# A conv block and a mixture of experts on one core: expert 0 made the fixed first place, its weights split ahead, tile 0 gathered by mask matmuls from rows in SBUF

## What is computed

```python
x = x + conv_block(ln_c(x))       # 8 x 256 x 16 x 16; groups of 8 channels: gates, 3x3 conv, FFT magnitude, sigmoid
t = to_tokens(x)                  # 2048 tokens x 256
xt = ln_t(t)
S = sigmoid(xt @ Wg)              # 2048 x 8
G, I = top_k(S, 2)
h = gelu(xt @ W1[e] + b1[e])      # 256 -> 1024, for each token's two experts e
y = h @ W2[e] + b2[e]             # 1024 -> 256
t = t + sum over the two experts of G * y
```

## Time and profile before

| | us |
|---|---|
| median of 3 runs (380.83 to 382.59) | 382.37 |
| the profiled execution | 382.42 |
| its span, first to last instruction | 380.2 |
| PE busy | 317.8 (84%) |
| DVE busy | 255.7 (67%) |
| ACT busy | 180.8 (48%) |
| POOL busy | 169.8 (45%) |

### The profile page before, as it was taken

How to read it: one execution, slowest core, us unless ns; L and a number is a source line. 1 busy time by engine, 2 the same in 40 slices (tenths; PEclk the granted TensorE clock), 3 DMA queues, 4 the chain that set the end, 5 groups by cost and what they waited for, 6 DMA issues and landing times.

```text
span 380.2 us, 8711 instructions
## 1 busy us (share of the span) xinstructions
PE 317.8 (84%) x3114; PEld 243.8 (64%) x3114; DVE 255.7 (67%) x572; ACT 180.8 (48%) x486; POOL 169.8 (45%) x145
## 2 busy tenths in 40 slices
PE   1899995999913109899999999999999999999960
PEld 1677631457713109788888888887888888888830
DVE  3986599437799552678878877887887656555640
ACT  3355583615429632654564466456456433442420
POOL 7023292514009451036456655654565555444331
PEclk9989998999955555999999999999999999999995
DMA  7300000001222986346676666767775444344221
GB/s 245 103 1 3 0 0 3 0 28 55 71 69 93 299 193 211 121 91 159 157 182 178 155 172 181 171 137 171 184 167 108 77 87 62 72 80 73 32 31 22
DMA packets 36696, 40.32 MB, mean 106 GB/s; under 512 B 8400, under 2 KB 33232, under 8 KB 36656
## 3 DMA queue, kind: packets, MB, share of 16 engines
q1 hardware_dynamic: 29168, 29.56, 27.2%
q0 software_dynamic: 7488, 10.23, 15.7%
HBM read 30.20 MB, written 9.57 MB: 105 GB/s over the span
## 4 chain that ended last, share of the span: by engine, by line
PE 47%; DMA 28%; DVE 11%; issue 4%; POOL 3%; ACT 3%; POOLq 0%; SPq 0%; ACTq 0%; DVEq 0%
DMA out<-fb,idx 21%; PE ps L839 9%; PE ps L828 5%; PE ps L832 5%; PE ps L830 5%; PE ps L840 5%; PE ps L673 4%; DMA fb<-xn_rows,idx 4%; POOL wt L437 3%; PE ps L693 3%; PE ps L702 2%; DMA xt<-x_tok 2%; PE ps L706 2%; PE ps L709 2%; DMA xn_rows<-wt 2%
## 5 line engine op out<-in xcount | busy, mean ns | idle before, releaser
L628 ACT ACTIVATE fb<-ps,b1t 128x128 f32<-128x128 f32 x312 | 84.7, 384 | 104.8 <-issue 101.5
L828 PE MATMUL ps<-fb,wt 128*128 128x128 f16 x624 | 121.9, 221 | 1.6 <-DVE fb L1202 1.6
L830 PE MATMUL ps<-fb,wt 128*128 128x128 f16 x624 | 121.9, 221 | 0.0
L832 PE MATMUL ps<-fb,wt 128*128 128x128 f16 x624 | 121.9, 221 | 0.0
L496 POOL DMA_INDIRECT out<-fb,idx x39 | 74.4, 1908 | 101.6 <-DMA out<-fb,idx 56.0
L839 PE MATMUL ps<-wt,fb 128*128 x312 | 117.5, 379 | 1.4 <-DVE fb L1202 1.4
L840 PE MATMUL ps<-wt,fb 128*128 x312 | 85.0, 273 | 0.0
L828 PEld LDWEIGHTS ps<-fb,wt 128*128 x624 | 61.8, 99 | 32.3 <-issue 1.8
L830 PEld LDWEIGHTS ps<-fb,wt 128*128 x624 | 61.8, 99 | 3.0
L832 PEld LDWEIGHTS ps<-fb,wt 128*128 x624 | 61.8, 99 | 0.0
L486 POOL DMA_INDIRECT fb<-xn_rows,idx x39 | 43.8, 1122 | 26.2 <-issue 9.8
(11 more groups left out here) (186 smaller groups left out, 401.4 us busy)
## 6 DMA issues: line engine op xcount, KB each, us to landing
wt<-w SPq DMA_DIRECT2D x32, 512.0 KB
b2t<-b SPq DMA_DIRECT2D x39, 128.0 KB
xt<-x_tok SPq DMA_DIRECT2D x4, 512.0 KB, 7.7
out<-xt SPq DMA_DIRECT2D x8, 256.0 KB, 2.1
xn_rows<-wt SPq DMA_DIRECT2D x8, 256.0 KB, 2.1
b1t<-params SPq DMA_DIRECT2D x39, 4.0 KB
fb<-xn_rows,idx POOLq DMA_INDIRECT x39
out<-fb,idx POOLq DMA_INDIRECT x39, 4.7
```

What stands on the lines that cost most here:

```text
L628: a = nc.scalar.activation(hid[:, s, f * P:(f + 1) * P], h_ps(s)[:, f * P:(f + 1) * P], ACT.Gelu_apprx_tanh, bias=b1t[:, n % NBIAS, f:f + ...
L828: pe.matmul(dst, hi, xT[:, s, c * P:(c + 1) * P], start=(c == 0 and f % 4 == 0), stop=False, skip_group_check=True)
L830: pe.matmul(dst, hi, xT[:, s, (2 + c) * P:(3 + c) * P], start=False, stop=False, skip_group_check=True)
L832: m = pe.matmul(dst, lo, xT[:, s, c * P:(c + 1) * P], start=False, stop=(c == DC - 1), skip_group_check=True)
```

## The change

- Expert 0 gets the highest sort key (`keybase`) and at least one tile, so place 0 is always expert 0, and tile 0 is always its first tile. Its four quarters and the biases of tile 0 are loaded at the start, from fixed addresses, and split in the conv stage. The second expert's first two quarters are split ahead of tile 0's gelu and of the gates' payload.
- The row blocks b = 0 and 1 are normalized inside the conv loop; the roots are taken in three parts (`ROWS_AT`) instead of two.
- Tile 0 is not gathered by DMA: DVE makes a mask per token block (`first`), PE multiplies the rows in SBUF by it, and the product is the transposed tile.
- `hot` and `pay` are made per block and choice by `tensor_scalar` with a scalar per partition; they are laid out so that PE reads 128 and 40 contiguous columns. Only one index table is made (40 columns instead of 80).
- The gate table moves from before step 0 to before step 2, `texp` gets a semaphore of its own, and POOL waits for `t_out` only before its first add.

```diff
-FIRST = SLOTS_MOST // P // E
+PLACE_FROM = [0] + [1 + -(-(SLOTS_MOST // P - 1) * p // (E - 1)) for p in range(E - 1)]
-QUARTERS_FIRST = QUARTERS
-QUARTERS_AHEAD = QUARTERS + 1
+QUARTERS_EARLY = QUARTERS + DC
-LATE_ROWS = B - 2
+ROWS_AT = [0, 3, B - 1, B]
+AHEAD = 4096.0
...
         def quarters_at(n):
-            first = QUARTERS_FIRST if n == 0 else n + QUARTERS_AHEAD
-            return range(first, min(n + QUARTERS_AHEAD + 1, NQ))
+            ahead = [4, 7, 8] + list(range(10, NQ + 1))
+            return range(ahead[n], ahead[n + 1]) if n + 1 < len(ahead) else range(0)
... SP
-            for b in range(B):
+            for h in range(QUARTERS):
+                load(h)
+            biases(0)
+            for b in range(B - 1):
                 sp.wait_ge(t_done, b + 1)
                 sp.dma_start(out_rows[:, 2 * b:2 * b + 2, :], xt[:, 2 * b:2 * b + 2, :]).then_inc(t_out, 16)
-            for b in range(B - NSTG + 1):
+            for b in range(B - 3):
                 rows_out(b)
+            sp.wait_ge(t_done, B)
+            sp.dma_start(out_rows[:, 2 * B - 2:2 * B, :], xt[:, 2 * B - 2:2 * B, :]).then_inc(t_out, 16)
             sp.wait_ge(perm_done, 1)
-            for h in range(NSTG):
+            for h in range(QUARTERS, QUARTERS_EARLY):
                 load(h)
-                if h + 1 < NSTG:
-                    rows_out(B - NSTG + 1 + h)
-            sp.wait_ge(table_done, 2)
-            for i in range(NBIAS):
+            for b in range(B - 3, B):
+                rows_out(b)
+            for h in range(QUARTERS_EARLY, 2 * QUARTERS):
+                load(h)
+            sp.wait_ge(texp_done, 1)
+            for i in range(1, NBIAS):
                 biases(i)
... POOL
-            g.tensor_scalar(by_row, c16[:, C16["iota"]].unsqueeze(2).broadcast_to([P, P, NBLK]), -1.0, 0.0,
-                            ALU.mult, ALU.add).then_inc(tables_set, 1)
-            for i in range(LEAD):
+            for i in range(1, LEAD):
                 gather(i)
... ACT
             deviation(grs[:, :], gmv[:, :, 1], eps_g, dev_g)
+            for h in range(DC):
+                split_hi(h)
...
             for u in range(B):
                 sigmoids(u)
                 if u in (0, 1, 4, 5):
                     shift(u + 4 if u < 2 else u + 2)
-            deviations(0, LATE_ROWS)
-            for b in range(LATE_ROWS - 1):
+                if DC <= u < QUARTERS:
+                    split_hi(u)
+                if u == B - 3:
+                    deviations(0)
+                if B - 3 <= u < B - 1:
+                    rows_hi(u - B + 3)
+            deviations(1)
+            for b in range(2, B - 1):
                 rows_hi(b)
-            deviations(LATE_ROWS, B - LATE_ROWS)
-            for b in range(LATE_ROWS - 1, B):
-                rows_hi(b)
+            deviations(2)
+            rows_hi(B - 1)
             act.wait_ge(logit_done, 2)
             nc.scalar.activation(sgl[:, :, :], lg[:, :, :], ACT.Sigmoid).then_inc(sigl_done, 1)
-            for h in range(QUARTERS_FIRST):
-                split_hi(h)
... PE
+            for k in range(NBLK):
+                if k % 4 == 0:
+                    pe.wait_ge(first_done, k // 4 + 1)
+                pe.wait_ge(xlo_done, k + 1)
+                for c in range(4):
+                    m = pe.matmul(ps[:, 0, c * P:(c + 1) * P], xrow[:, k, c * P:(c + 1) * P], first[:, k, :],
+                                  start=(k == 0 and c == 0), stop=(k == NBLK - 1), skip_group_check=True)
+            m.then_inc(xT_mm, 1)
-            table(0, 7)
-            pe.wait_ge(table_done, 2)
+            table(1, 1, 7)
...
-            turn(0)
-            load_expert(0)
-            table(2, 6)
+                if n == 0:                       # at the end of step(n)
+                    pe.wait_ge(texp_done, 1)
+                    load_expert(1)
+                    turn(1)
             for n in range(TILES + 2):
+                if n == 2:
+                    table(2, 2, 6)
                 step(n)
... DVE
+                if b < QUARTERS:
+                    split_lo(b)
                 if 2 <= b <= B:
                     add_x(b - 2)
                     stats_t(b - 2)
+                if b == B - 3:
+                    invert(0)
+            invert(1)
...
-            invert(0, LATE_ROWS)
             dve.wait_ge(prefix_mm, 1)
...
+            for k in range(NBLK):
+                ins = v.tensor_scalar(first[:, k, :], iota16, lowest[:, k:k + 1], None, ALU.is_equal)
...
             for a in range(TOP_K):
-                v.tensor_tensor(out=hot[:, a], in0=by_row, in1=place16[:, 0, a].unsqueeze(1).broadcast_to([P, P, NBLK]),
-                                op=ALU.is_equal).then_inc(hot_done, 1)
-            invert(LATE_ROWS, B - LATE_ROWS)
+                for k in range(NBLK):
+                    q = a * NBLK + k
+                    v.tensor_scalar(hot[:, q, :], iota16, minus_row[:, a, k:k + 1], 0.0, ALU.add, ALU.is_equal)
+                    ins = v.tensor_scalar(pay[:, q, 1, :], tiles16, tile_of[:, a, k:k + 1], cc("token")[:, k:k + 1],
+                                          ALU.is_equal, ALU.mult)
+                ins.then_inc(hot_done, 1)
+                if a == 0:
+                    invert(2)
+            rows_T(0)
             dve.wait_ge(table_mm, 1)
... idx, texp, scaled logits as before
-            for h in range(QUARTERS_FIRST):
+            for h in range(QUARTERS, QUARTERS_EARLY):
                 split_lo(h)
...
+            over_tiles = lambda n: place16[:, n].rearrange("p a k -> p (a k)").unsqueeze(2).broadcast_to([P, 2 * NBLK, TCOL])
+            link(v.tensor_tensor(out=pay[:, :, 0, :], in0=tiles16.unsqueeze(1).broadcast_to([P, 2 * NBLK, TCOL]),
+                                 in1=over_tiles(1), op=ALU.is_equal))
             for n in (2, 3):
-                ins = v.tensor_tensor(out=pay[:, n], in0=pay[:, 0], in1=over_tiles(place16[:, n]), op=ALU.mult)
+                ins = v.tensor_tensor(out=pay[:, :, n, :], in0=pay[:, :, 0, :], in1=over_tiles(n), op=ALU.mult)
```

More of the change, by code:

```diff
@@ L212, in build @@
         slot = sb("slot", [P, NBLK, E])
-        pick = view(1664, 2 * NBLK * E).rearrange("p (a k e) -> p a k e", a=2, k=NBLK)
+        pick, picked = [late[:, at:at + 2 * NBLK * E].rearrange("p (a k e) -> p a k e", a=2, k=NBLK) for at in (2880, 3136)]
         psum_pick = sb("picked", [P, 2, 2, NBLK])
@@ L216, in build @@
         place16 = sb("place16", [P, 4, 2, NBLK], F16)
-        tok16 = sb("tok16", [P, 2, NBLK], F16)
-        texpf = view(1920, TCOL * E).rearrange("p (i e) -> p i e", e=E)
+        keybase = sb("keybase", [P, E])
+        steps_of = view(4960, E * NBLK).rearrange("p (e k) -> p e k", k=NBLK)
+        lowest = view(5088, NBLK)
+        near, tile_of, minus_row = [view(at, 2 * NBLK).rearrange("p (a k) -> p a k", a=2) for at in (5104, 5136, 5168)]
+        texpf = late[:, 2560:2560 + TCOL * E].rearrange("p (i e) -> p i e", e=E)
         texpc = sb("texpc", [P, TCOL])
@@ L585, in rows_hi @@
             def rows_hi(b):
-                act.wait_ge(trs_done, 1 if b < LATE_ROWS else 2)
+                act.wait_ge(trs_done, 1 + (b >= ROWS_AT[1]) + (b >= ROWS_AT[2]))
                 for k in (2 * b, 2 * b + 1):
@@ L804, in step @@
                 one, two = n < TILES, n >= 2
-                if n % FIRST == 0 and n < FIRST * E:
-                    pe.wait_ge(lo_done, QUARTERS * (n // FIRST + 1))
-                if one:
+                for p in range(E):
+                    if n == PLACE_FROM[p]:
+                        pe.wait_ge(lo_done, QUARTERS_EARLY if p == 1 else QUARTERS * (p + 1))
+                if n == PLACE_FROM[1] + 2:
+                    pe.wait_ge(lo_done, 2 * QUARTERS)
+                e1 = e2 = 0
+                if one and n > 0:
                     e1 = pe.snap(expert[n % UNROLL], min_val=0, max_val=E - 1)
-                if two:
+                if n > 2:
                     e2 = pe.snap(expert[(n - 2) % UNROLL], min_val=0, max_val=E - 1)
@@ L818, in step @@
                 for f in range(FC):
-                    for c in range(DC if one else 0):
+                    for c in range(DC if one and n > 0 else 0):
                         pe.lower_ap(piece(e1, c * F + f * P + P - 1, 1))
                         pe.lower_ap(piece(e1, PIECE + c * F + f * P + P - 1, 1))
-                    if two:
+                    if n > 2:
                         pe.lower_ap(piece(e2, 2 * PIECE + f * 2 * C, 2 * C))
@@ L1071, in stats_t, with invert @@
                 ins.then_inc(var_t, 1)
-            def invert(b, n):
-                dve.wait_ge(dev_t, 1 if b == 0 else 2)
-                at = slice(2 * b, 2 * (b + n))
+            def invert(part):
+                dve.wait_ge(dev_t, part + 1)
+                at = slice(2 * ROWS_AT[part], 2 * ROWS_AT[part + 1])
                 link(v.reciprocal(trs[:, at], trs[:, at]))
@@ L1185, in _ @@
-            ins.then_inc(hot_done, 1)
+            slots = psum_pick[:, 0]
```

(15 more changed lines are left out.)

154 lines of the change are left out of this document (78 added, 76 removed).

## The result

| | before | changed |
|---|---|---|
| median of 20 runs each, same chip | 380.02 us (377.77 to 382.6) | 385.19 us |
| ratio, 95% interval | | 1.0119 [1.0097, 1.0141] |
| the profiled execution | 382.42 | 384.68 |
| its span | 380.2 | 382.4 |

The changed kernel is 1.2% slower by the ratio (1.4% by the medians). The forecast was 381.1 us, range 374.5 to 385.5, with 0.41 on faster and 0.27 on slower: its sign was wrong, and the time is near the top of the range. (The ratio leaves out two of the changed kernel's runs, one of 578.83 us at a granted clock of 0.557 and one of 390.27; the median of its other 18 is 384.9.)

What follows compares the result with a forecast made beforehand. PE was taken as full from step 2 on, so only time before it counts: -1.0 us at step 2 and -0.3 from the start, from the median 382.37 to 381.1 us; range 374.5 to 385.5.

Steps and rivals of the forecast that it cites:

- The conv stage and its loop: End of conv loop: extra ACT work delays L1096 by 3.2 us; what follows moves by 2.65 us.
- The slots: DVE's routing ahead of the masks: forecast at 117.85 us, before at 115.12.
- The masks: DVE's masks for tile 0 and the tables: 0.165 us per 128-wide mask, +8.9 us in sum.
- pairs: DVE's two 40-wide table masks with two scalars each: 0.37 us together, sixteen such in 5.9 us.
- products: DVE's three 1280-wide gate products ahead of step 1: 1.4 us each, +2.6 us in sum.
- B: Masks on DVE are cheap, 0.10 us each: total 374.6 to 376 us, chance 0.24.
- D: Two-scalar masks on DVE are dear, 0.32 us each: total 384.8 us, chance 0.09.
- Step 0, step 1: PE's first tile steps: step 0 at 136.1 us, twelve earlier; step 1 at 149.5, released by DVE's copy, before 153.33.
- Rival E: Tile 1's gather lands after 153 us, so step 1 starts no earlier: total 384.9 us, chance 0.05.
- Step 1, gate table, step 2: On PE: step 1 takes 5.3 us, gate table 2.2; the mark, step 2's start, at 157.0 against 158.0 before.
- Rival C: PE's clock is low at the gate table and early step 2: total 386.3 us, chance 0.12.
- The tables on ACT: Two new table switches in the conv loop at 1.28 us each, no drain; the skill's rule would give 383.9 total.

Runs made afterwards that it cites:

- e1: The kernel before, run again with no edit for a second profile: 379.99 us, ratio 0.9985.
- e9: The changed kernel with POOL's wait for `t_out` ahead of the first add alone: 380.83 us, ratio 1.0003 to the kernel before.
- e3: The kernel before without adds, tile results written by SP to rows of their own: 371.16 us, ratio 0.9741.
- e4: The changed kernel without adds, tile results written by SP to rows of their own: 372.02 us, ratio 0.9758 to the kernel before.
- e10: The kernel before with the wait for `t_out` added to every add, its early one kept: 387.79 us, ratio 1.0188.
- e2: The changed kernel, run again with no edit for a second profile: 384.25 us, ratio 1.0101 to the kernel before.
- e5: The changed kernel with DVE waiting once, at iteration 27, for the add of two tiles before: 388.25 us, ratio 1.0192 to the kernel before.

## Why the prediction was wrong, step by step

**Where it starts.** The forecast is made against a profiled execution of 382.42, near the median of the three runs shown. Twenty runs gave 380.02, and the profiled execution of e1 took 379.67. Of the 2.75 us between the two profiles 2.1 stand at step 2, where the gather of tile 0 took 5.18 instead of 8.07 us, and 0.7 in the tile of 6.17 us that e1 doesn't have. So up to two of the us that the change was to save were the scatter of one row (8.07, 5.18, 7.81 and 8.33 us in four profiles). I had bounded the price of each edit and not the scatter of the row that the whole gain comes from.

**The conv stage and its loop.** L1137 was forecast at 109.05 and came at 109.79. The slots, forecast at 117.85, came at 119.96 + 0.42 = 120.4 (L1183): some of DVE's operations with two tensor inputs take 0.66 instead of the 0.29 of L1105 before (L1146 above), 1.8 us in all. POOL, idle before up to 113.7 us, now works from 110.6 us on; that it is the cause is argued from this alone. I had priced its company for the masks and not for these.

**The masks** were right: 0.165 from start to start forecast, 2.68 / 16 = 0.17 measured; pairs 0.37 and 0.37; products 1.4 and 1.45. Rivals B and D fall. On what the Trainium skill (VectorE: DVE Perf Modes, section The perf-mode tier table) gives the elements these rows say no more: 0.17 us holds the cost of the scalar as well.

**Step 0, step 1.** Forecast 136.1 and 149.5, measured 137.43 and 150.89, step 1 released by DVE's copy as said. The slots were 2.5 us late and step 0 only 1.3, since I had taken 0.107 us for each of the index table's last 16 matmuls, of 40 columns, and the sixteen took 0.72 together. Rival E falls.

**Step 1, gate table, step 2.** Forecast 5.3 and 2.2 us, measured 155.16 - 150.89 = 4.3 and 1.1. The granted clock over these stretches of the changed kernel (us, length, busy time by engine, clock, DMA share, GB/s):

```profile
150.90:153.70 2.80, 2.80 (x27) 2.80 (x28) 1.85 (x3) 0.00 (x0) 0.00 (x0) 0.50 0.22 34
153.70:156.30 2.60, 2.60 (x60) 2.60 (x58) 2.50 (x3) 0.88 (x4) 0.00 (x0) 0.99 0.53 174
156.30:160.00 3.70, 3.70 (x53) 3.06 (x50) 2.26 (x5) 3.19 (x8) 0.00 (x0) 1.00 0.00 0
```

Full clock was back 2.8 us into step 1, sooner than the five us that I took from step 0 of before, and the table found it high. Rival C falls. Step 2 came at 156.30, forecast 157.0. That the mark came out so near is in part luck: 2.5 us late at the slots, 1.1 early in the index table, 1.0 in step 1 and 1.1 in the gate table.

**The tables on ACT.** In the changed kernel the load of 139.69 lasts 1.28 us and the next activation starts at its end, as in the earlier trace rows:

```profile
139.69 1.28 ACT L634 ACT_TABLE_LOAD   x1
140.98 0.20 ACT L634 ACTIVATE scrap<-eps 128x1 f32<-128x1 f32 x1
```

The two new loads in the conv loop, at 96.19 and 100.17, are the same: 1.28 us each, and ACT goes on 0.01 behind. No drain of 1.38 shows. The total of 383.9 by the rule of the Trainium skill (ScalarE: Activation LUTs, section What ACT_TABLE_LOAD costs) would have been near the measured time for a wrong reason.

**The step that failed** is this sentence: "What lies behind it, 380.2 - 158.0 = 222.2 us, I leave as it is (39 tiles before and after, the same matmuls in each)." The matmuls are indeed the same. The adds are not: each has a wait more. In the profiled pair the stretch behind tile 1's result grew by 1.69 + 2.31 us (the table above), and taking the wait out again gives 385.19 - 380.83 = 4.4 us between the medians of the changed kernel and e9 (in different groups of runs; by ratios 1.0119 against 1.0003, the same 1.2%). The sentence before it, that a microsecond is won only before step 2 because PE is full from there on, failed with it. The profile had the warning: 21% of its chain stood in the adds (the rows from 164.69 above), and POOL sat idle for 56.0 us until an add had landed (`out<-fb,idx` at L496, in the list of costliest groups). The prediction has no word on the adds and doesn't ask how much room they had. Up to tile 23 it was next to none: there the adds of that execution start 5.51 us apart on average, as far as the tiles. And I read the move of the wait as one of place, not of count.

**What the tail does.** With e9 the change's own worth can be read: 1.0003 [0.9978, 1.0028], no measurable gain, where the forecast had 1.3 us. That fits e3 and e4. Results of tile 1 in four profiles of each form (e1, e3, e10 and the first; e2, e4, e9 and the first) average 169.6 before and 168.6 after; this 1.0 us is below what a comparison of this kernel tells (the four of before alone lie between 168.0 and 171.4).

## Carry to other kernels

When a wait moves into a loop, count the waits of the instruction that it lands on: a satisfied wait isn't free, and on an instruction that is nearly paced by its own predecessor it decides the time. Ask of every repeated transfer not only whether it is hidden but with how much room per turn: here, with two waits, a few tenths of a us of 5.5, and 0.5 us of gap more used them up. And take a second profile of the kernel before pricing a gain that rests on one DMA's latency: 8.07 and 5.18 us are the same transfer.

## What the runs showed of the hardware that I had not expected

**A third wait.** On POOL's indirect DMA two waits give a gap of 0.27 us from landing to start and three give 0.78. Both kernels have a piece of its own on POOL's sequencer ahead of these DMAs, at the line of the wait for `y_done`. Count and duration in ns (min/median/max), before and changed:

```profile
L495 POOLq EVENT_SEMAPHORE  x38: 17/17/17, 170.2 to 370.1; - x38
L508 POOLq EVENT_SEMAPHORE  x39: 17/1931/3427, 163.6 to 370.1; - x39
```

Before, the piece takes 17 ns each time: it waits for `y_done` alone, and the DMA itself waits for the landing. In the changed kernel it takes up to 3.4 us and ends with the landing: by the trace's records it carries the waits for `y_done` and `add_out`, and the DMA is left with `t_out`. So the satisfied wait, written first, stands where the one that matters stood. What a wait ahead costs is seen at the very first add, which no landing holds. Before, it waits for `y_done` alone, has no such piece, and starts 0.27 us behind the result (164.69 above); in the changed kernel it waits for `t_out` too:

```profile
163.56 0.02 POOLq L508
163.57 0.81 issue
164.38 6.28 DMA out<-fb,idx
```

The 0.8 us by which the adds in time follow DVE's result in every kernel are the same price: there the result is what the piece waits for. That it would be enough to write the wait for `t_out` last follows from this reading; no run tests it. The Trainium skill, Perfetto Trace Analysis, section Identifying Dependency Chains, says that an instruction which waits on several engines may have further wait conditions in separate instructions ahead of it. The trace agrees with that; the price is the runs'.

**Issue beside DVE.** DVE's 1024-wide pass with two inputs in the changed kernel, beside the adds of 337.08 and 342.84:

```profile
336.92 1.23 DVE L1253 SCALAR_TENSOR_TENSOR fb<-fb 128x1024 f16<-128x1024 f32 x1
...
342.42 1.23 DVE L1253 SCALAR_TENSOR_TENSOR fb<-fb 128x1024 f16<-128x1024 f32 x1
```

The pass ends at 338.15 and 343.65, and the issues end at 339.60 and 345.11: 1.45 and 1.46 us behind it. It is so throughout: 35 of the 39 issues of the changed kernel start inside this pass or inside a weight split (L906, 1.22 us, also with two inputs), and 34 of them end 1.43 to 1.47 us behind the end of the pass in which they start. The one left starts 0.01 us behind the start of its pass and isn't stretched. An issue that starts ahead of the pass (e9 at 339.66, its pass at 340.56) takes 1.59. The Trainium skill, SBUF — State Buffer, section SBUF: two separate sides, says that a DVE operation with two SBUF inputs and a GpSimd operation that reads SBUF exclude each other, and whichever starts first keeps the port for its whole length. The issues that start second agree. The other half doesn't show: the pass of e9 at 340.56 starts while the issue runs (to 341.25) and takes 1.23 us as elsewhere. The two states of e5 would follow from the first half: a late issue is stretched by some 0.9 us (2.5 instead of 1.59), and with three waits an add that long leaves no room to catch up. No kernel tested it by itself.
